# Retention heads with Strassen's scheme: another order of DVE's, ACT's and PE's work, and a weight ring whose slots follow one rule

## The chip, the cores and the metric

The kernel runs on one core of a Trainium2 chip. The metric is the device time of one execution in microseconds, the median over several executions. In the profile PE is TensorE (matmuls), DVE is VectorE, ACT is ScalarE, SP is SyncE (which issues the DMAs).

## The reference

One decoder layer in float32 over x of 8 x 100 tokens by 1024, with a context of 722 tokens for each of the 8 batches. Three parts follow one another, each with a residual and a layer norm: retention, cross attention with its own keys and the context's, and a feed-forward of 4096. The change touches retention alone:

```python
q, k = rope(x @ Wq), rope(x @ Wk)            # 8 heads of 128
v, g = x @ Wv, x @ Wg                        # 8 heads of 256
scores = einsum('bihd,bjhd->bhij', q * scale, k) * D    # D: causal decay of the head
o = einsum('bhij,bjhd->bihd', scores, v)
o = o * rsqrt(mean(o * o) + EPS) * g_norm_weight        # over a head's 256
o = o * (g * sigmoid(g))
x = layernorm(x + o.reshape(B, T, 2048) @ Wo)
```

## The kernel before, in words

Everything is held with its features in the partitions and the 800 tokens side by side. Each float32 operand is split into a high part, rounded by ACT, and a low part, value minus high part, made by DVE. A product is then three matmuls for each 128 x 128 piece of weights: high by high, high by low, low by high.

`phase_retention` works through eight heads. Head 0 (`first_head`) and head 7 (`last_head`) multiply by plain units: 1024 x 128 weights by all 800 tokens, 48 matmuls, in two column parts of 512 and 288. Heads 1 to 6 (`head(i)`) take the weights of q and k, of v, and of g as three blocks (j = 0, 1, 2) of 1024 x 256, and multiply each by Strassen's scheme with seven products (`product(i, j, p)`, p = 0 to 6) over quarters of 512 x 128 weights and 400 tokens, 12 matmuls each. To this belong:

- **Sides.** Four of the seven moving operands are sums of quarters of x. They are made once, in the first head and at the start of head 1: `side_sum(n)` on DVE (L1207), `side_hi(n)` on ACT (L917), `side_lo(n)` on DVE (L1212). Product 1 uses side 2, product 2 side 1, product 3 side 3 and product 5 side 4. Side 4 lies where the upper right quarter of x was (`operand(0, 1)`), so that quarter is restored for head 7, by loading it again (tile QKR), a copy on ACT (L1077) and a low part on DVE (L1449).
- **Weights.** `mix` (DVE, L1165) makes the four weight sums of a block. `entry_hi` (ACT, L878) and `entry_lo` (DVE, L1133) split one quarter of weights into a slot of a ring of four, which is the same memory as the two plain slots WH and WL. An entry is numbered e: 25 to a head, of which 7 for q and k, 7 for v, 4 of the output weights, 7 for g. Its copy waits until PE is done with the entry that had the slot before. From entry 139 (the first output weights of head 6) on, the slots are shifted by two, and entries 139 and 140 wait for entries 137 and 138.
- **Combinations.** PE adds some products up in PSUM; `keep` (ACT, L897), `first_quarter` (ACT, L910) and `combine` (DVE, L1191) make the four quarters of the result: u2, u3, c22, c21, c12, in this order. Their semaphore is `outs`. Product 3 waits for u2, product 5 for u3, product 6 for c22.
- **The head's output.** `weigh_rows` lies between matmuls of block 2. ACT squares and scales the rows (`token_squares` L957, `scaled_rows` L969), PE turns them back (`turn_back`, L1595), DVE multiplies by norm and gate (`gated_output`, L1320), ACT and DVE split (L951, L1310). All of this belongs to head i - 1 and runs at the start of head i. `project_output` (PE, L1519 to L1521) multiplies by the output weights, eight tiles n, through two pairs of PSUM banks; from n = 2 on it waits until DVE's `add_output` (L1260) has added tile n - 2 to the residual R.
- **Rotations** of q and k: `rotate_cos` (L1233), `rotate_sin` (L1238), `rotate_sum` (L1246), between the products of block 1.

Each engine executes its own list in the order in which it is written; nothing is reordered. The order of `head` in `vector` is therefore what decides which of DVE's results comes first: for i > 1 it reads c12 of the head before, low parts 3 and 4, mix 3, u2, low part 5, mixes 0 and 1 of block 1, low part 6, gated output, u3, c22. Before that, at the end of head i - 1, stand low parts 0, 1 and 2.

In the last head PE first waits for c12 of head 6 (`outs`), then runs the first unit (L1723 to L1725) into banks 0 and 1, for each column part first the four pieces of x's lower half and then the four of the restored upper half. On DVE the restored low part (L1449) stands ahead of c12.

Of the kernel before, what the change touches and what calls it, by code (L numbers as in the profile page):

```python
# [682 lines left out]
def phase_retention(c, nc, sem, before, norm):  # L683


    with ExitStack() as ctx:
# [59 lines left out]
        JUMP = PER * (STRASSEN - 1) + OUTPUT_ENTRY  # L746
# [3 lines left out]
        def slot(e):  # L750
            return (e + (2 if e >= JUMP else 0)) % RING

        def slot_users(e):

            return e - 2 if JUMP <= e < JUMP + 2 else e - 4

# [106 lines left out]
        def scalar(act):  # L863
            def plain_hi(u):
                split_hi(c, act, u)

            def entry_hi(e, source, pair, sums):

                before_it = slot_users(e)
                if before_it < 0:  # L870
                    act.wait_ge(c.unit_done, 5 if e < 2 else 6)
                else:
                    act.wait_ge(f_done, F_DONE + before_it + 1)
# [39 lines left out]
            def side_hi(n):  # L913
                act.wait_ge(t_sum, T_SUM + n)
                if n == 3:
                    act.wait_ge(c.unit_done, 6)
# [59 lines left out]
            def first_head():  # L976
# [5 lines left out]
                for t in range(2):  # L982
                    plain_hi(U_RET + WV + t + 2)
# [10 lines left out]
                token_squares(0, 1)  # L994
                act.wait_ge(c.unit_done, 6)
# [18 lines left out]
            def head(i):  # L1014
# [5 lines left out]
                if i == 1:  # L1020
                    side_hi(4)
                    side_hi(3)
# [6 lines left out]
                output_hi(i - 1)  # L1029
                product_hi(i, 1, 0)  # L1030
                first_quarter(i, 0)
                product_hi(i, 1, 1)
# [35 lines left out]
                root(i)  # L1068
                scaled_rows(i)
# [3 lines left out]
            def last_head():  # L1073
                i, u = END, U_END_HEAD
                act.wait_ge(x_back, X_BACK + 16)
                act.wait_ge(f_done, F_DONE + LAST_ENTRY)
                act.activation(operand(0, 1)[0], F1, ACT.Copy).then_inc(t_hi, 1)  # L1077
# [42 lines left out]
        def vector(dve):  # L1120
# [4 lines left out]
            def plain_lo(u):  # L1125
                split_lo(c, dve, u)

# [39 lines left out]
            def combine(i, j, which):  # L1167
# [10 lines left out]
                if which == "u2":  # L1178
                    dve.wait_ge(kept, KEPT + m + 1)
                    if j == 0:  # L1180
                        dve.wait_ge(t_lo, T_LO + 4)
# [27 lines left out]
            def side_lo(n):  # L1209
                dve.wait_ge(t_hi, T_HI + {1: 1, 2: 2, 4: 3, 3: 4}[n])  # L1210
# [114 lines left out]
            def first_head():  # L1325
# [4 lines left out]
                for t in range(2):  # L1330
                    plain_lo(U_RET + WV + t + 2)
# [10 lines left out]
                product_lo(1, 0, 1)  # L1342
                side_lo(2)
                side_sum(4)
                side_sum(3)
# [3 lines left out]
            def head(i):  # L1349
                if i > 1:  # L1350
                    combine(i - 1, 2, "c12")
                    product_lo(i, 0, 3)
                    product_lo(i, 0, 4)
                    mix(i, 0, 3)
                    combine(i, 0, "u2")
                    product_lo(i, 0, 5)
                    mix(i, 1, 0)
                    mix(i, 1, 1)
                    product_lo(i, 0, 6)
                    gated_output(i - 1)  # L1360
                else:
                    product_lo(i, 0, 4)
                    mix(i, 0, 3)
                    side_lo(4)
                    side_lo(3)
                    combine(i, 0, "u2")
                    gated_output(i - 1)
                    product_lo(i, 0, 5)
                    mix(i, 1, 0)
                    mix(i, 1, 1)  # L1370
                    product_lo(i, 0, 6)
                combine(i, 0, "u3")
                combine(i, 0, "c22")
# [12 lines left out]
                mix(i, 1, 3)  # L1386
                rotate_sin(i, 0, 0)
                combine(i, 1, "u2")
# [54 lines left out]
                if i < STRASSEN:  # L1443
                    product_lo(i + 1, 0, 2)

            def last_head():
                i, u = END, U_END_HEAD
                dve.wait_ge(t_hi, T_HI + 5)
                dve.tensor_tensor(operand(0, 1)[1], F1, operand(0, 1)[0].bitcast(F32),  # L1449
                                  ALU.subtract).then_inc(t_lo, 1)  # L1450
                combine(STRASSEN, 2, "c12")
# [60 lines left out]
        def tensor(pe):  # L1512
# [109 lines left out]
            def product(i, j, p):  # L1622
# [23 lines left out]
                if m == 0 and p in (1, 2, 3, 5):  # L1646
                    pe.wait_ge(t_lo, T_LO + {1: 2, 2: 2, 5: 3, 3: 4}[p])
# [24 lines left out]
            def first_head():  # L1672
# [16 lines left out]
                weights(u + WG)  # L1689
                unit_matmuls(c, pe, 0, 6, XH, XL)  # L1690
                weights(u + WG + 1)
                pe.wait_ge(s_masked, 1)
                unit_matmuls(c, pe, 1, 0, XH, XL,
                             lambda h, k: weigh_rows(0, k) if h == 0 else None)

            def head(i):
                for p in range(PRODUCTS):
                    product(i, 0, p)
                    if p == 2:
# [1736 lines left out]
```

## Time and profile before

| | |
|---|---|
| runs | 2728.45, 2728.88, 2729.19 us; median 2728.88 |
| profiled execution | 2728.11 us; its span from first to last instruction 2726.3 us |
| mean granted clock of TensorE | 0.995 of full speed |
| busy DVE, ACT | 62%, 43% of the span |
| retention | from about 550 us to 1152 us of the span |

The rows further down come from several views. The page gives the busy time of each engine. The table of waits says which engine waited for whose result, with the sum, the count and the longest. The view by stretch gives busy time with the number of instructions, the granted clock, and what the DMAs moved. A timeline lists an engine's instructions in the order of time: start, duration, engine, line, operation, output <- inputs, shapes, count; in square brackets the time for which the engine idled just before it, and whom it then waited for.

### The profile page before, as it was taken

What the parts mean: (1) busy time and instruction counts of PE and PEld (TensorE: products, weight loads), DVE (VectorE), ACT (ScalarE), POOL (GpSimd) and SP (SyncE); (2) the same over time, 40 slices, a digit from 0 to 9 for tenths busy, and PEclk for the clock granted to TensorE, in tenths of its full rate; (3) what the DMA queues carried; (4) which work ended last, traced back from release to release, by engine and by line L of the source; (5) the groups of instructions that cost most, each with busy time, mean ns of one, the idle gap of its engine ahead of it and who ended that gap; (6) DMA issues with size and microseconds to landing.
All of it is one profiled execution on the core that took longest, in us unless ns stands there. A gap on an engine that the chain in (4) does not pass through costs nothing. (4 is left out here: it accounts for less than half of the span.)

```text
span 2726.3 us, 39732 instructions
## 1 busy us (share of the span) xinstructions
PE 2666.2 (98%) x15130; PEld 2480.9 (91%) x15130; DVE 1701.0 (62%) x2369; ACT 1162.8 (43%) x2036; POOL 0.9 (0%) x9
## 2 busy tenths in 40 slices
PE   8999999999999998999999999999999999999997
PEld 7888888988999998998889999989999998999997
DVE  4333333368777776558778888845983673773767
ACT  4344444444444443335456666632541341431432
POOL 0000000000000000000000000000000000000000
PEclk9999999999999999999999999999999999999999
DMA  5433333421111111206125555522121121121222
GB/s 209 131 131 131 131 131 131 172 74 56 55 63 63 63 47 59 78 31 143 62 96 167 170 168 168 156 60 99 62 78 62 62 78 62 62 78 49 76 89 100
DMA packets 117224, 265.98 MB, mean 98 GB/s; under 512 B 19822, under 2 KB 86254, under 8 KB 102894
## 3 DMA queue, kind: packets, MB, share of 16 engines
q1 hardware_dynamic: 117102, 264.31, 30.3%
q8 instruction: 82, 1.34, 0.2%
q14 instruction: 40, 0.33, 0.0%
HBM read 206.63 MB, written 57.66 MB: 97 GB/s over the span
## 5 line engine op out<-in xcount | busy, mean ns | idle before, releaser
L129 PE MATMUL PS<-XH,WH 128*128 128x512 f32 (+1 forms) x624 | 215.4, 345 | 0.5 <-DVE t_ROOM L2960 0.4
L131 PE MATMUL PS<-XH,WL 128*128 128x512 f32 (+1 forms) x624 | 215.4, 345 | 0.0
L2816 ACT ACTIVATE WH<-RAW 128x512 fp32r<-128x512 f32 x180 | 113.3, 631 | 222.1 <-PE PS L2692 119.8
L444 PE MATMUL PS<-CH,KWH 128*128 128x338 f32 (+1 forms) x512 | 167.8, 328 | 12.4 <-DVE CL L420 12.4
L3049 DVE TENSOR_TENSOR WL<-RAW,WH 128x512 fp32r<-128x512 f32 x196 | 134.8, 688 | 58.5 <-ACT WH L2816 55.2
L130 PE MATMUL PS<-XL,WH 128*128 128x512 f32 (+1 forms) x496 | 170.1, 343 | 0.0
L445 PE MATMUL PS<-CL,KWH 128*128 128x338 f32 (+1 forms) x512 | 167.6, 327 | 0.0
L446 PE MATMUL PS<-CH,KWL 128*128 128x338 f32 (+1 forms) x512 | 167.5, 327 | 0.0
L2690 PE MATMUL PS<-XL,WH 128*128 128x400 f32 x480 | 166.0, 346 | 0.0
L2688 PE MATMUL PS<-XH,WH 128*128 128x400 f32 x480 | 164.8, 343 | 0.8 <-issue 0.6
L2692 PE MATMUL PS<-XH,WL 128*128 128x400 f32 x480 | 165.1, 344 | 0.0
L2418 DVE TENSOR_TENSOR XL<-PS,XH 128x400 fp32r<-128x400 f32 (+2 forms) x224 | 122.6, 571 | 58.2 <-ACT XH L2357 53.9
L89 ACT ACTIVATE WH<-RAW 128x1024 fp32r<-128x1024 f32 x57 | 60.4, 1061 | 230.9 <-PE PS L131 178.1
L368 DVE TENSOR_TENSOR VS<-PS,VS 128x512 fp32r<-128x512 f32 (+1 forms) x48 | 33.1, 689 | 191.0 <-ACT VS L282 191.0
L470 PE MATMUL PS<-VWH,CL 128*128 128x512 f32 (+1 forms) x384 | 150.0, 391 | 0.0
L469 PE MATMUL PS<-VWH,CH 128*128 128x512 f32 (+1 forms) x384 | 150.0, 391 | 0.0
L471 PE MATMUL PS<-VWL,CH 128*128 128x512 f32 (+1 forms) x384 | 149.6, 390 | 0.0
L2357 ACT ACTIVATE XH<-PS 128x400 fp32r<-128x400 f32 (+2 forms) x224 | 106.2, 506 | 99.2 <-PE PS L2268 97.4
L95 DVE TENSOR_TENSOR WL<-RAW,WH 128x1024 fp32r<-128x1024 f32 x58 | 70.9, 1224 | 121.7 <-ACT WH L89 117.3
L878 ACT ACTIVATE WH<-RAW 128x512 fp32r<-128x512 f32 x132 | 81.7, 633 | 126.1 <-PE PS L1662 69.7
L2725 PE MATMUL PS<-t_ROOM,WL 128*128 128x512 f32 (+1 forms) x384 | 132.5, 345 | 0.0
L2401 DVE TENSOR_REDUCE a_LOW<-PS 100x1 f32<-100x824 f32 x128 | 129.8, 1014 | 4.2 <-PE PS L2257 1.6
(404 smaller groups left out, 7610.8 us busy)
## 6 DMA issues: line engine op xcount, KB each, us to landing
RAW<-weights_dram SPq DMA_DIRECT2D x111, 1024.0 KB, 4.9
values_scratch<-VS SPq DMA_DIRECT2D x40, 512.0 KB, 7.2
a_KHL<-keys_scratch SPq DMA_DIRECT2D x32, 411.0 KB, 5.0
keys_scratch<-KS SPq DMA_DIRECT2D x16, 768.0 KB, 6.2
R<-context_dram SPq DMA_DIRECT2D x8, 1352.0 KB, 6.8
keys_scratch<-KS SPq DMA_DIRECT2D x16, 676.0 KB, 5.5
R<-context_dram SPq DMA_DIRECT2D x7, 1536.0 KB, 6.9
XH<-values_scratch SPq DMA_DIRECT2D x16, 640.0 KB
```

The source lines that it names most:

```text
L129: pe.matmul(out, wh, xh[:, k, cols], start=(k == 0), stop=False)
L130: pe.matmul(out, wh, xl[:, k, cols], start=False, stop=False)
L131: mm = pe.matmul(out, wl, xh[:, k, cols], start=False, stop=(k == KT - 1))
L444: pe.matmul(out, wh, CH[e][:, k, 0:w], start=(k == 0), stop=False)
L445: pe.matmul(out, wh, CL[e][:, k, 0:w], start=False, stop=False)
L446: mm = pe.matmul(out, wl, CH[e][:, k, 0:w], start=False, stop=(k == KT - 1))
L469: pe.matmul(out, ch, vwh[:, k, :], start=(k == 0), stop=False)
L470: pe.matmul(out, cl, vwh[:, k, :], start=False, stop=False)
L471: mm = pe.matmul(out, ch, vwl[:, k, :], start=False, stop=(k == KT - 1))
L2688: pe.matmul(out, wh, high[:, k, :], start=(OPENS[p] and k == 0), stop=False, skip_group_check=True)
L2690: pe.matmul(out, wh, low[:, k, :], start=False, stop=False, skip_group_check=True)
L2692: mm = pe.matmul(out, wl, high[:, k, :], start=False, stop=(k == QUAD - 1), skip_group_check=True)
```

## The change

- **First head.** ACT and DVE split the two gate units in the other order, unit 1 into slot 0 first, unit 0 into slot 1 second. PE multiplies by unit 0 from slot 1 first and waits for both. Side 3's sum comes ahead of side 2's low part, its copy ahead of the second gate's activation, its low part still in the first head.
- **Ring.** Slots are (e + 2) mod 4 for all entries, and each entry waits for the one four before it.
- **Head 1.** u2 is DVE's first operation. Side 4's low part is the only one left. Then low part 5, u3, c22, the gated output, mixes 0 and 1 of block 1, low part 6. PE turns head 0's output back after product 3, no longer after product 2. ACT copies that output later.
- **Heads 2 to 6.** c12 of the head before comes ahead of low part 2. The gated output follows u2, and then come low part 5, u3, c22, the mixes, low part 6. In block 1 u2 comes ahead of the first half of `rotate_sin`.
- **Last head.** ACT copies the restored quarter between the root and the scaling of head 6's rows. DVE makes c12 ahead of the restored low part. PE runs the unit's four pieces that need nothing restored first, right columns (bank 1) and then left ones (bank 0), waits for c12 only ahead of the left ones, and then the four restored pieces in the same order.

Context is shortened here.

```diff
@@ -743,16 +743,11 @@
         LAST_ENTRY = PER * STRASSEN - 1
-        JUMP = PER * (STRASSEN - 1) + OUTPUT_ENTRY
         ring = [x[:].rearrange("p u (s w) -> p (u s) w", s=2) for x in (c.WH, c.WL)]
...
         def slot(e):
-            return (e + (2 if e >= JUMP else 0)) % RING
-
-        def slot_users(e):
-
-            return e - 2 if JUMP <= e < JUMP + 2 else e - 4
+            return (e + 2) % RING
 
@@ -864,13 +859,19 @@
 
+            def first_gate_hi(t):
+
+                u = U_RET + WG + t
+                act.wait_ge(c.raw[(u // 2) % 2], raw_count(u // 2))
+                act.wait_ge(c.unit_done, WG - t)
+                act.activation(c.WH[:, 1 - t, :], raw_unit(c, u), ACT.Copy).then_inc(c.w_hi, 1)
+
             def entry_hi(e, source, pair, sums):
 
-                before_it = slot_users(e)
-                if before_it < 0:
+                if e < RING:
                     act.wait_ge(c.unit_done, 5 if e < 2 else 6)
                 else:
-                    act.wait_ge(f_done, F_DONE + before_it + 1)
+                    act.wait_ge(f_done, F_DONE + e - RING + 1)
                 if sums is not None:
@@ -912,7 +913,7 @@
                 act.wait_ge(t_sum, T_SUM + n)
-                if n == 3:
+                if n == 4:
                     act.wait_ge(c.unit_done, 6)
@@ -980,7 +981,7 @@
                 for t in range(2):
-                    plain_hi(U_RET + WV + t + 2)
+                    first_gate_hi(1 - t)
                     act.activation(halves(VT[:, t, :]), row800(c, 4 + 2 * t),
@@ -992,6 +993,7 @@
                 token_squares(0, 1)
+                side_hi(3)
                 act.wait_ge(c.unit_done, 6)
@@ -1019,16 +1021,18 @@
                     side_hi(4)
-                    side_hi(3)
                 else:
...
                 product_hi(i, 0, 6)
-                output_hi(i - 1)
+                if i > 1:
+                    output_hi(i - 1)
                 product_hi(i, 1, 0)
                 first_quarter(i, 0)
+                if i == 1:
+                    output_hi(i - 1)
                 product_hi(i, 1, 1)
@@ -1066,15 +1070,16 @@
                 root(i)
+                if i == STRASSEN:
+                    act.wait_ge(x_back, X_BACK + 16)
+                    act.wait_ge(f_done, F_DONE + LAST_ENTRY)
+                    act.activation(operand(0, 1)[0], F1, ACT.Copy).then_inc(t_hi, 1)
                 scaled_rows(i)
...
                 i, u = END, U_END_HEAD
-                act.wait_ge(x_back, X_BACK + 16)
-                act.wait_ge(f_done, F_DONE + LAST_ENTRY)
-                act.activation(operand(0, 1)[0], F1, ACT.Copy).then_inc(t_hi, 1)
                 plain_hi(u + 1)
@@ -1125,6 +1130,11 @@
 
+            def first_gate_lo(t):
+                dve.wait_ge(c.w_hi, U_RET + WG + 2 - t)
+                dve.tensor_tensor(c.WL[:, 1 - t, :], raw_unit(c, U_RET + WG + t),
+                                  c.WH[:, 1 - t, :].bitcast(F32), ALU.subtract).then_inc(c.w_lo, 1)
+
             def entry_lo(e, source):
@@ -1178,7 +1188,7 @@
                     if j == 0:
-                        dve.wait_ge(t_lo, T_LO + 4)
+                        dve.wait_ge(t_lo, T_LO + 3)
                     if j == 1:
@@ -1207,7 +1217,7 @@
             def side_lo(n):
-                dve.wait_ge(t_hi, T_HI + {1: 1, 2: 2, 4: 3, 3: 4}[n])
+                dve.wait_ge(t_hi, T_HI + n)
                 high, low = side(n)
@@ -1328,7 +1338,7 @@
                 for t in range(2):
-                    plain_lo(U_RET + WV + t + 2)
+                    first_gate_lo(1 - t)
                 mask_scores(0)
@@ -1340,37 +1350,37 @@
                 product_lo(1, 0, 1)
+                side_sum(3)
                 side_lo(2)
                 side_sum(4)
-                side_sum(3)
+                side_lo(3)
                 product_lo(1, 0, 2)
...
                     combine(i - 1, 2, "c12")
+                    product_lo(i, 0, 2)
                     product_lo(i, 0, 3)
...
                     combine(i, 0, "u2")
+                    gated_output(i - 1)
                     product_lo(i, 0, 5)
-                    mix(i, 1, 0)
-                    mix(i, 1, 1)
-                    product_lo(i, 0, 6)
-                    gated_output(i - 1)
+                    combine(i, 0, "u3")
+                    combine(i, 0, "c22")
                 else:
+                    combine(i, 0, "u2")
                     product_lo(i, 0, 4)
...
                     side_lo(4)
-                    side_lo(3)
-                    combine(i, 0, "u2")
+                    product_lo(i, 0, 5)
+                    combine(i, 0, "u3")
+                    combine(i, 0, "c22")
                     gated_output(i - 1)
-                    product_lo(i, 0, 5)
-                    mix(i, 1, 0)
-                    mix(i, 1, 1)
-                    product_lo(i, 0, 6)
-                combine(i, 0, "u3")
-                combine(i, 0, "c22")
+                mix(i, 1, 0)
+                mix(i, 1, 1)
+                product_lo(i, 0, 6)
                 product_lo(i, 1, 0)
@@ -1384,8 +1394,8 @@
                 mix(i, 1, 3)
+                combine(i, 1, "u2")
                 rotate_sin(i, 0, 0)
-                combine(i, 1, "u2")
                 product_lo(i, 1, 5)
@@ -1440,15 +1450,13 @@
                 combine(i, 2, "c21")
-                if i < STRASSEN:
-                    product_lo(i + 1, 0, 2)
 
...
                 i, u = END, U_END_HEAD
+                combine(STRASSEN, 2, "c12")
                 dve.wait_ge(t_hi, T_HI + 5)
...
                                   ALU.subtract).then_inc(t_lo, 1)
-                combine(STRASSEN, 2, "c12")
                 plain_lo(u + 1)
@@ -1644,7 +1652,7 @@
                 if m == 0 and p in (1, 2, 3, 5):
-                    pe.wait_ge(t_lo, T_LO + {1: 2, 2: 2, 5: 3, 3: 4}[p])
+                    pe.wait_ge(t_lo, T_LO + {1: 2, 2: 2, 3: 3, 5: 4}[p])
                 if e == LAST_ENTRY:
@@ -1686,17 +1694,16 @@
                 turn(0)
-                weights(u + WG)
-                unit_matmuls(c, pe, 0, 6, XH, XL)
                 weights(u + WG + 1)
+                unit_matmuls(c, pe, 1, 6, XH, XL)
                 pe.wait_ge(s_masked, 1)
-                unit_matmuls(c, pe, 1, 0, XH, XL,
+                unit_matmuls(c, pe, 0, 0, XH, XL,
                              lambda h, k: weigh_rows(0, k) if h == 0 else None)
...
                     product(i, 0, p)
-                    if p == 2:
+                    if p == (3 if i == 1 else 2):
                         turn_back(i - 1)
@@ -1711,18 +1718,20 @@
                 weights(u)
-                pe.wait_ge(outs, OUTS + 5 * 3 * STRASSEN)
-                restored = [4, 5, 6, 7, 0, 1, 2, 3]
-                for h in range(2):
-                    cols = slice(*PARTS[h])
-                    out = c.PS[:, h, 0:PARTS[h][1] - PARTS[h][0]]
-                    for n, k in enumerate(restored):
-                        if n == 4:
+                for restored in (False, True):
+                    for h in (1, 0):
+                        if not restored and h == 0:
+                            pe.wait_ge(outs, OUTS + 5 * 3 * STRASSEN)
+                        if restored and h == 1:
                             pe.wait_ge(t_lo, T_LO + 5)
-                        wh, wl = (x[:, u % 2, k * P:(k + 1) * P] for x in (c.WH, c.WL))
-                        pe.matmul(out, wh, XH[:, k, cols], start=(n == 0), stop=False)
-                        pe.matmul(out, wh, XL[:, k, cols], start=False, stop=False)
-                        mm = pe.matmul(out, wl, XH[:, k, cols], start=False, stop=(n == KT - 1))
+                        cols = slice(*PARTS[h])
+                        out = c.PS[:, h, 0:PARTS[h][1] - PARTS[h][0]]
+                        for k in range(0, QUAD) if restored else range(QUAD, KT):
+                            wh, wl = (x[:, u % 2, k * P:(k + 1) * P] for x in (c.WH, c.WL))
+                            pe.matmul(out, wh, XH[:, k, cols], start=(k == QUAD), stop=False)
+                            pe.matmul(out, wh, XL[:, k, cols], start=False, stop=False)
+                            mm = pe.matmul(out, wl, XH[:, k, cols], start=False,
+                                           stop=(k == QUAD - 1))
                 mm.then_inc(c.unit_done, 1)
```

## Rows read from the trace of the kernel before

**Rows 1.** The page: busy time, share of the span and instructions of each engine.
```profile
PE 2666.2 (98%) x15130; PEld 2480.9 (91%) x15130; DVE 1701.0 (62%) x2369; ACT 1162.8 (43%) x2036; POOL 0.9 (0%) x9
```
**Rows 2.** PE's waits, whole span: for whom, us in total, times, longest.
```profile
PE PS L1658 <- DVE QKR L1191: 6.9, 6, 4.7
PE PS L1723 <- DVE G L1191: 5.0, 1, 5.0
PE PS L1519 <- DVE R L1260: 3.3, 1, 3.3
...
PE PS L1658 <- DVE W L1191: 2.3, 5, 0.5
PE PS L1859 <- DVE h_SQL L2025: 2.3, 1, 2.3
...
PE PS L1658 <- DVE G L1191: 1.3, 5, 0.3
```
**Rows 3.** Busy time by stretch: length, PE, PEld, DVE, ACT, POOL, clock, DMA share, GB/s.
```profile
620.00:622.00 2.00, 0.00 (x0) 0.00 (x0) 2.00 (x2) 1.27 (x3) 0.00 (x0) 0.51 0.00 0
...
627.13:649.09 21.96, 21.96 (x121) 21.82 (x121) 19.96 (x29) 8.48 (x14) 0.00 (x0) 1.00 0.29 97
...
1022.00:1024.00 2.00, 0.00 (x0) 0.00 (x0) 1.97 (x4) 0.34 (x1) 0.00 (x0) 1.00 0.00 0
...
1077.69:1103.91 26.22, 26.22 (x148) 23.15 (x146) 16.06 (x16) 6.36 (x8) 0.00 (x0) 1.00 0.12 41
...
1412.00:1414.00 2.00, 2.00 (x8) 1.66 (x7) 1.66 (x3) 1.97 (x3) 0.00 (x0) 0.50 0.75 285
```
**Rows 4.** Timeline of DVE, head 1.
```profile
618.84 1.82 DVE L1212 TENSOR_TENSOR XL<-T,XH 128x1600 fp32r<-128x1600 f32 x1
...
622.53 0.57 DVE L1191 TENSOR_TENSOR QKR<-U,PS 128x400 f32<-128x400 f32 x1
623.02 2.00 DVE L1320 SCALAR_TENSOR_TENSOR G<-PS,GNW,G 128x800 f32<-128x800 f32 x2
...
628.64 0.68 DVE L1133 TENSOR_TENSOR WL<-RAW,WH 128x512 fp32r<-128x512 f32 x1
...
637.14 0.69 DVE L1133 TENSOR_TENSOR WL<-RAW,WH 128x512 fp32r<-128x512 f32 x1 [0.77 <-ACT WH L878]
```
**Rows 5.** Timeline of DVE, head 2.
```profile
697.02 0.69 DVE L1133 TENSOR_TENSOR WL<-RAW,WH 128x512 fp32r<-128x512 f32 x1 [2.72 <-ACT WH L878]
...
703.03 0.69 DVE L1133 TENSOR_TENSOR WL<-RAW,WH 128x512 fp32r<-128x512 f32 x1 [0.31 <-ACT WH L878]
...
725.88 0.98 DVE L1260 TENSOR_TENSOR R<-R,PS 128x800 f32<-128x800 f32 x1
```
**Rows 6.** Timeline of PE: turn backs, third projection tile of head 2.
```profile
616.91 1.59 PE L1595 MATMUL PS<-ID,W 100*128 100x100 f32 x16 [0.59 <-ACT W L969]
...
695.72 1.54 PE L1595 MATMUL PS<-ID,W 100*128 100x100 f32 x16
...
727.01 0.47 PE L1519 MATMUL PS<-VHL,WH 128*128 128x512 f32 x1
...
1076.38 0.85 PE L1595 MATMUL PS<-ID,W 100*128 100x100 f32 x8
```
**Rows 7.** Timeline of DVE, output weights of head 6.
```profile
1015.52 0.69 DVE L1133 TENSOR_TENSOR WL<-RAW,WH 128x512 fp32r<-128x512 f32 x1 [3.19 <-ACT WH L878]
```
**Rows 8.** Timelines of DVE and ACT, start of the last head.
```profile
1062.55 1.83 DVE L1449 TENSOR_TENSOR XL<-QKR,XH 128x1600 fp32r<-128x1600 f32 x1 [3.20 <-ACT XH L1077]
1064.29 0.56 DVE L1191 TENSOR_TENSOR G<-G,PS 128x400 f32<-128x400 f32 x1
...
1058.07 3.02 ACT L969 ACTIVATE W<-PS,RSS 100x256 f32<-100x256 f32 x8
1060.93 1.58 ACT L1077 ACTIVATE XH<-QKR 128x1600 fp32r<-128x1600 f32 x1
```

## The prediction

> **What bounds the kernel now.** I read the page first, then the table of PE's waits, then the busy time by stretch, and last the timelines of single engines around each wait. The page [rows 1] says that PE is busy 98% of the span, so only its idle time, or time at a lower clock, can be won: the change removes no matmul. The table of waits [rows 2] puts 18.8 us of that idle time in retention, in five rows: 6.9 us at L1658 for QKR (six waits, the longest 4.7), 5.0 once at L1723 (the last head), 3.3 once at L1519 (the output projection), 2.3 in five small waits for W and 1.3 in five for G. Clock: in the stretches [rows 3] the granted clock is 0.51 (its 1.2 GHz level) right after the long wait of head 1 and 1.00 (2.4 GHz) in the middle of the 3.3 us wait. So the 4.7 and 5.0 us waits also cost time at half clock.
>
> The second thing to see is in the DVE timeline: between a head's turned-back output and its first row sums (L1260) DVE works nearly without a gap. In head 2 the first such sum ends at 725.88 + 0.98 = 726.86 [rows 5] and the third projection matmul group starts at 727.01 [rows 6], 0.15 later, which is the latency of a semaphore. So **once per head DVE's queue, not PE, sets the time**. Small PE waits removed before that point come back there, unless DVE also gets there earlier. I assume that head 1 and heads 3 to 6 are alike; the code of that stretch is the same.
>
> **Head 1.** The third product ends at 616.91 - 0.59 = 616.32 [rows 6]. PE then turns head 0's output back (1.59 us) and waits 4.7 us, up to 623.2, since product 3 needs u2, which DVE makes at 622.53 behind the low parts of side 4 (618.84) and side 3 [rows 4]. The new order makes side 3's sum, high and low part inside the first head, ahead of the low part of entry 2, which there waits for ACT's second gate; I price that at nothing, and at one low part (1.82 us) if this cover were gone. u2 comes first in the head. Product 3 then starts at 616.3 at once and the turn back follows it. The stretch from product 4's start at 627.13 holds ten products in 21.96 us [rows 3], 2.2 each (product 3, at half clock, took 627.13 - 623.2 = 3.9 or 4.0: 1.8 more). Now PE ends product 3 at 618.5, the turn back at 620.0, product 4 at 622.2 and product 5 at 624.4. DVE: side 4's low part starts at 618.84 as before. Side 3's is gone from there (622.53 - 618.84 - 1.82 = 1.87 us), and so is u2 (623.02 - 622.53 = 0.49). The operations up to the next block's first low part are otherwise the same ones in another order, so that one starts at 628.64 - 2.36 = 626.3. The low part of product 6 stands right before it, behind the gated output and two mixes, and PE has wanted it since 624.4: **a new wait of 1.9 us**. Later the 0.77 us that DVE idled for ACT at 637.14 [rows 4] goes too, because ACT's copy there follows PE's product, which now ends some 5 us earlier. DVE reaches the first row sum 2.36 + 0.77 = 3.1 us earlier, and PE, which has more in hand than that, waits there. Term: **3.1 us**, out of the 0.6 + 4.7 + 1.8 = 7.1 that the waits and the clock cost; PE keeps 7.1 - 1.9 - 3.1 = 2.1 us in hand at the row sum.
>
> **Heads 2 to 6.** The third quarter of the block before (c12) is put ahead of a low part, which removes PE's 0.26 us wait for G (1.3 in five) [rows 2]. The turn back of head 2 ends at 695.72 + 1.54 = 697.26 [rows 6], so now at 697.0. The gated output now starts there instead of the low part of product 5, which waited for ACT until 697.02 [rows 5]. Up to the low part at 703.03 the operations are the same ones, without the 0.31 us idle before it, as the gated output is finished sooner and ACT's copies of it with it. DVE gains 0.31 + 0.04 = 0.35 us per head, 5 x 0.35 = **1.75 us**. That u3 no longer stands behind the gated output (6.9 - 4.7 = 2.2 in five, 0.44 us of PE's wait per head, in the QKR row) and u2 no longer behind a rotation (0.46, the W row) I price at nothing: this time comes back at the row sum, which covers it. Were that cover gone, it would be 0.44 + 0.46 per head, 4.5 in five.
>
> **Ring without a skip.** Slots are now (entry + 2) mod 4 throughout. Before, entries 14 and 15 of head 6 had to wait for the product two entries back. DVE idled 3.19 us for that at 1015.52 [rows 7] and PE waited 3.3 us at L1519 [rows 2]. Both go: **3.3 us**. To match, the first head's two gate units change slots, with copies and low parts at the same places behind the same waits, but PE now wants both before the first. No row shows that wait. Its bounds are 0 and one low part, which is at most the 1.82 us of the longer one at 618.84 [rows 4]; I take 0, as the scores and transposes lie between the second low part and the gates on PE.
>
> **Last head.** PE ends the Strassen products at about 1060.0: c12 ends at 1064.29 + 0.56 = 1064.85 [rows 8], 0.15 of latency, less the 5.0 us wait. Its restored unit then runs to 1076.38 [rows 6], 16.4 us in all, where three units of this shape take 26.22 us [rows 3], 8.74 each. After the change nothing holds PE: the halves over the unrestored rows stand first, the first of them in a bank that nobody still reads, so it starts at 1060.0. The second needs c12, which DVE now makes as soon as the last product ends (about 1060.7), as it no longer queues behind L1449. The restored part needs L1449's result. ACT's copy for it now stands ahead of the scaling (1058.07, 3.02 us), so it is done by 1058.07 + 1.58 = 1059.7, and DVE's by 1060.7 + 1.83 = 1062.5, while PE has half of 8.74 us of work up to 1064.4. The scaling ends by 1062.7, and the turn back wants it at 1068.7. Term: 16.4 - 8.7 = **7.7 us**, 5.0 of them wait and 2.7 clock.
>
> **Other moved steps.** SyncE's load of the output weights waits for the low part of product 6, which in heads 2 to 6 is made some 3 us later, behind the gated output. Seven products (15 us) lie between that and the copies that need it, so I take 0; its bounds are 0 and the 0.77 us for which DVE idled for a copy in rows 4, per head. The load of the next pair and the copies of the gated output move with DVE.
>
> **Sum.** 3.1 + 1.75 + 3.3 + 7.7 = 15.85 us, against the profiled execution's 2728.1 (span 2726.3 and 1.8 around it): 2712.3. The median of the runs is 0.8 higher, so the forecast is **2713.0 us**, -0.6%. About 0.2% (5.5 us) is what a measurement of this kernel can tell from no change.
>
> **Rivals.**
> *The clock falls at the new wait of head 1.* A 2.3 us wait at L1859 [rows 2] was followed by a clock of 0.50 in the stretch from 1412 [rows 3], while the 3.3 us wait of head 6 was not. So 1.9 us can do it. Half clock cost PE 1.8 us in head 1 and 2.7 in the last head, where a full product or unit ran through it; I take up to 3.5 for a drop whose whole length is filled with work. PE has 2.1 us of that in hand before the row sum: 1.4 us, 2714.4. Chance 0.22.
> The Trainium skill's page "TensorE: Matmul & The Clock Gate", Part 1 ("What's actually happening"), says that the monitor behind the clock runs freely and doesn't restart with the kernel. By that a wait near 2 us may or may not lower the clock from run to run; no row here repeats one wait in two executions.
> *All waits go.* DVE keeps up and PE gets back 18.8 us and the clock's 1.8 and 2.7: 23.3 us, 2705.6. Against it speaks the gapless DVE queue up to 726.86. Chance 0.08.
> *The ring gives nothing* because head 6 waits for something else at the same place (the row sums), or the part does not act: 2716.3, and 2720 if c12 also stays late in the last head. Chance 0.09.
> *Slower.* In heads 2 to 6 the low parts of products 5 and 6 now queue behind the gated output, which waits for the turn back and for ACT's gates. Product 6's low part is ready at about 702.7 and PE wants it at 696.8 + 3 x 2.2 = 703.4: 0.7 us in hand. If the gates or the turn back come late, each microsecond past 0.7 is PE's wait in five heads, and the clock may fall as well (1.8 each time, as in head 1). Late by 3 us: 5 x (2.3 + 1.8) = 20.5 us, 2733; slower than before from about 2.2 us on. Against it: ACT finished the copy that the row at 697.02 waited for by then, and the gates stand ahead of that copy on ACT, so they are done some microseconds before 697.0. Chance 0.04.
>
> **How the numbers follow.** The forecast has 0.57. Its own unknowns (0.35 per head by +-0.3, the head 1 term by +-1, latencies) make 2710.5 to 2715.5. The range takes in the clock rival and the missing ring, and half the way to "all waits go": 2708 to 2718. Faster by over 0.2% holds for all cases but the slower one and mishaps in between: 0.93, within 0.2% 0.03, slower 0.04.
>
> **What would show it.** Right: no wait at L1723; no 4.7 us wait, but one of about 2 us at L1658 in head 1 whose releaser is a low part (L1133); new waits at L1519 for R (L1260) of 0.5 to 0.9 us in each of six heads, in place of QKR and W; a granted clock of 1.00 all through the last head's first unit. Wrong: L1519 without waits (then more was won), a wait before product 6 in every head, or waits in the last head's unit.

## The result, and the profile after

The changed kernel takes **2709.01 us** in the median of four runs (2708.18 to 2709.96), the one before 2729.03 (2728.45 to 2729.31): 20.0 us less, ratio 0.9927, 95% interval 0.9910 to 0.9944. The profiled executions stand at 2728.11 and 2709.04, their spans at 2726.3 and 2707.2.

Of after, first the engines in the page, then PE's waits in the whole span (for whom, us in total, times, longest):
```profile
PE 2660.4 (98%) x15130; PEld 2476.9 (91%) x15130; DVE 1700.3 (63%) x2369; ACT 1162.6 (43%) x2036; POOL 0.9 (0%) x9
```
```profile
PE PS L444 <- DVE CL L420: 12.6, 1, 12.6
PE PS L1527 <- DVE R L1270: 2.5, 5, 0.5
...
PE PS L1666 <- DVE WL L1143: 2.1, 1, 2.1
...
PE PS L1666 <- DVE W L1201: 1.0, 5, 0.2
```
The instruction counts are those of [rows 1]; nothing was removed. The first row lies outside retention. Of retention's 18.8 us in [rows 2], 5.6 are left, in the other three rows: the waits for QKR and G are gone, head 6's 3.3 us wait for R has become one of five of 0.5 us, the waits for W are shorter, and a wait for WL is new. DVE releases all of them. Lines have moved: L1133 is L1143 now, L1191 L1201, L1260 L1270, L1519 L1527, L1658 L1666, L1723 L1731.

The time is best followed from one first row sum to the next, since that operation occurs once per head. DVE's timeline after:
```profile
614.14 0.57 DVE L1201 TENSOR_TENSOR QKR<-U,PS 128x400 f32<-128x400 f32 x1
...
618.78 1.83 DVE L1222 TENSOR_TENSOR XL<-T,XH 128x1600 fp32r<-128x1600 f32 x1
622.28 2.00 DVE L1330 SCALAR_TENSOR_TENSOR G<-PS,GNW,G 128x800 f32<-128x800 f32 x2
...
625.53 1.29 DVE L1143 TENSOR_TENSOR WL<-RAW,WH 128x512 fp32r<-128x512 f32 x2
...
648.98 0.98 DVE L1270 TENSOR_TENSOR R<-R,PS 128x800 f32<-128x800 f32 x1
...
693.49 2.01 DVE L1330 SCALAR_TENSOR_TENSOR G<-PS,GNW,G 128x800 f32<-128x800 f32 x2 [2.84 <-PE PS L1603]
...
698.50 1.29 DVE L1143 TENSOR_TENSOR WL<-RAW,WH 128x512 fp32r<-128x512 f32 x2
...
721.95 0.98 DVE L1270 TENSOR_TENSOR R<-R,PS 128x800 f32<-128x800 f32 x1
...
1013.68 0.98 DVE L1270 TENSOR_TENSOR R<-R,PS 128x800 f32<-128x800 f32 x1
...
1050.19 0.57 DVE L1201 TENSOR_TENSOR G<-G,PS 128x400 f32<-128x400 f32 x1 [0.70 <-PE PS L1670]
1050.68 1.82 DVE L1458 TENSOR_TENSOR XL<-QKR,XH 128x1600 fp32r<-128x1600 f32 x1
```
and PE's:
```profile
626.36 0.52 PE L1666 MATMUL PS<-XH,WH 128*128 128x400 f32 x1 [2.14 <-DVE WL L1143]
...
691.85 1.54 PE L1603 MATMUL PS<-ID,W 100*128 100x100 f32 x16
...
1049.99 0.29 PE L1731 MATMUL PS<-XH,WH 128*128 128x288 f32 x1
...
1058.71 0.34 PE L1603 MATMUL PS<-ID,W 100*128 100x100 f32 x2
```
For before, beside [rows 5, 6]:
```profile
652.35 0.98 DVE L1260 TENSOR_TENSOR R<-R,PS 128x800 f32<-128x800 f32 x1
```
The first row sums of heads 1 to 6 stood at 652.35, 725.88, 799.40, 872.97, 946.54 and 1023.55 before, and stand at 648.98, 721.95, 794.88, 867.82, 940.75 and 1013.68 after. From these and the first turn back of the last head (1076.38 before, 1058.71 after):

| stretch | before | after | gain | forecast |
|---|---|---|---|---|
| to row sum of head 1 | 652.35 | 648.98 | 3.37 | 3.1 |
| row sums 1 to 2, 2 to 3, 3 to 4, 4 to 5 | 73.53, 73.52, 73.57, 73.57 | 72.97, 72.93, 72.94, 72.93 | 0.56 to 0.64 | 0.35 each |
| row sums 5 to 6 | 77.01 | 72.93 | 4.08 | 0.35 + 3.3 |
| row sum 6 to last turn back | 52.83 | 45.03 | 7.80 | 7.7 |

These are 17.67 us. The other 1.4 of the span's 19.1 lie behind retention, where the change has no part, and they are luck: before, the granted clock fell once more near 1774; after, it did not. The changed kernel was profiled a second time ("The changed kernel once more", below), and there it did. Before, after, and the same place in that second execution (length, PE, PEld, DVE, ACT, POOL, clock, DMA share, GB/s):
```profile
1774.00:1776.00 2.00, 2.00 (x9) 1.78 (x9) 1.03 (x2) 0.80 (x2) 0.00 (x0) 0.50 0.91 46
```
```profile
1774.00:1776.00 2.00, 2.00 (x10) 1.66 (x9) 2.00 (x3) 0.00 (x0) 0.00 (x0) 1.00 0.00 0
```
```profile
1758.00:1760.00 2.00, 2.00 (x10) 1.86 (x9) 1.09 (x2) 0.72 (x2) 0.00 (x0) 0.50 0.91 70
```

### The profile page after: what moved, and what is told of

Same layout as the page of the kernel before. It is cut to its first block and busy times, and to the rows that moved or that the text cites. A ratio compares the mean times of both kernels' runs of the same rounds, so it can differ in the third digit from the quotient of the medians.

```text
span 2707.2 us, 39730 instructions
## 1 busy us (share of the span) xinstructions
PE 2660.4 (98%) x15130; PEld 2476.9 (91%) x15130; DVE 1700.3 (63%) x2369; ACT 1162.6 (43%) x2036; POOL 0.9 (0%) x9
```

## The experiments

### Four parts, one at a time, on the kernel before

**The last head alone**: c12 ahead of L1449's low part, ACT's copy ahead of the scaling, unrestored rows first. Of the edit only DVE's part is shown.
```diff
+                combine(STRASSEN, 2, "c12")
                 dve.wait_ge(t_hi, T_HI + 5)
                 dve.tensor_tensor(operand(0, 1)[1], F1, operand(0, 1)[0].bitcast(F32),
                                   ALU.subtract).then_inc(t_lo, 1)
-                combine(STRASSEN, 2, "c12")
```


> The kernel before with the last head's part alone: PE runs the unrestored pieces first, DVE makes c12 ahead of the restored low part, ACT copies the restored quarter ahead of the scaling. Theory (the last head's stall is local, all of it goes): -7.8 us against before, 2721.2, of which 5.0 is the wait at L1723 and the rest the clock; no clock of 0.5 around 1064. Rival (part of it comes back in the unit behind, for instance as a wait for the rotations or the turn back): -5 us or less, 2724. The stretches at half clock further down (at 1412 and 1774 in before) may come or go and are worth up to 1.7 us each.


Measured: 2723.77 us against 2729.07, ratio 0.9977 (0.9967 to 0.9986). The unit itself shrank to 8.72 us as forecast (1064.61 to 1073.33). But the profiled execution lost time elsewhere. Its busy time by stretch at head 6's 3.3 us wait for the row sums (columns as in [rows 3]):
```profile
1026.00:1028.00 2.00, 1.22 (x3) 1.05 (x4) 2.00 (x3) 1.16 (x2) 0.00 (x0) 0.50 0.00 0
1028.00:1030.00 2.00, 2.00 (x7) 1.61 (x7) 1.04 (x2) 0.00 (x0) 0.00 (x0) 0.50 0.88 225
```
The clock fell at a wait that had left it at 1.00 in the profiled execution of before [rows 3], and the way from that row sum to the unit's start took 38.96 us instead of 36.29 (before without its 5.0 us wait), 2.7 more. The ten runs form two groups, four at 2720.5 to 2721.4 and six at 2723.7 to 2724.8, some 3 us apart. That the upper group is the one whose clock falls there fits, but only one of the ten, of the upper group, has a trace.

**The ring alone**: slots (e + 2) mod 4, with the first head's gate units exchanged.
```diff
         def slot(e):
-            return (e + (2 if e >= JUMP else 0)) % RING
...
+            return (e + 2) % RING
```


> The kernel before with the ring without a skip and the swapped gate units alone. Theory (head 6 then behaves like heads 2 to 5): the 3.3 us wait at L1519 goes, head 6 takes 73.6 us from row sum to row sum in place of 77.0: -3.4 us, 2725.6. Rival (the row sums hold PE at the same place anyway, or the gate units cost a wait in the first head): 0 to -1 us.


Measured: 2724.80, ratio 0.9984 (0.9975 to 0.9994). The step to head 6's row sum is 73.54 instead of 77.01, **3.5 us** less, L1519's wait is gone, and the others stand as in [rows 2], these two among them:
```profile
PE PS L1664 <- DVE QKR L1197: 6.9, 6, 4.7
PE PS L1728 <- DVE G L1197: 5.0, 1, 5.0
```
The exchanged gate units show no wait. The median moved by 4.3, 0.8 more than this stretch. In the profiled execution the last head's unit and its half clock took 10.20 us from start to turn back (1063.33 to 1073.53) where before took 11.38 (1065.00 to 1076.38), with the same 5.0 us wait ahead: the length of a drop varies too.

**The first head alone**: side 3 made ahead, u2 first, PE's product 3 ahead of the turn back.
```diff
                 token_squares(0, 1)
+                side_hi(3)
...
                     side_hi(4)
-                    side_hi(3)
```


> The kernel before with head 1's part alone: sides in the order 1, 2, 3, 4 with side 3 in the first head, u2 first, turn back behind product 3, gated output behind c22. Theory (DVE's queue sets the time): the first row sum of head 1 comes 3.3 us earlier (649.0 in place of 652.35), with a wait of 2.1 us before product 6; -3.3 us, 2725.7. Rival (PE sets the time): the 4.7 and 0.6 us waits and the 1.8 us of half clock go, 2.1 come back: -5.0 us, 2724.


Measured: 2725.34, ratio 0.9987 (0.9978 to 0.9997). PE's first turn back and DVE's row sum:
```profile
618.73 0.25 PE L1601 MATMUL PS<-ID,W 100*128 100x100 f32 x1
...
649.42 0.98 DVE L1263 TENSOR_TENSOR R<-R,PS 128x800 f32<-128x800 f32 x1
```
They are 30.69 us apart, as after the whole change (618.29 to 648.98), with the same 2.1 us wait for WL.

**The order of heads 2 to 6 alone.**
```diff
                     combine(i - 1, 2, "c12")
+                    product_lo(i, 0, 2)
...
                     combine(i, 0, "u2")
+                    gated_output(i - 1)
                     product_lo(i, 0, 5)
+                    combine(i, 0, "u3")
+                    combine(i, 0, "c22")
                     mix(i, 1, 0)
                     mix(i, 1, 1)
                     product_lo(i, 0, 6)
-                    gated_output(i - 1)
...
```


> The kernel before with the order of heads 2 to 6 alone (and u2 ahead of the first rotation half in block 1 of every head). Theory (DVE's queue sets the time; the turn back comes 0.5 us earlier and DVE's 0.31 us idle time goes): heads 2 to 5 take 72.95 us each in place of 73.5, row sums wait 0.5 us at L1519; head 6 keeps its ring wait; -3.0 to -3.8 us, 2725.6. Rival (as forecast, 0.35 per head): -1.75 us. Rival (PE sets the time): 1.2 per head, -6 us.


Measured: 2726.23, ratio 0.9990 (0.9981 to 1.0000). Row sums are 72.94, 72.92, 72.94 and 72.93 apart, so this part alone gives the 0.6 us per head; head 6, still with its ring wait, takes 75.70 (77.01 before: 1.3 less). The 2.2 of QKR and 1.3 of G are gone, and 5.4 - 3.3 = 2.1 stand at the row sums:
```profile
PE PS L1520 <- DVE R L1260: 5.4, 5, 3.3
```
In this execution too the clock fell at head 6's 3.3 us wait:
```profile
1022.00:1024.00 2.00, 2.00 (x6) 1.52 (x6) 1.49 (x2) 0.00 (x0) 0.00 (x0) 0.50 0.69 131
```
The way from that row sum to the unit's start, without the 5.0 us wait ahead of it, took 38.97 us, 2.7 more than before, as with the last head alone. In the profiled execution of the first head alone, the fastest of its ten, the same wait left the clock at 1.00.

The four medians add to 5.3 + 4.3 + 3.7 + 2.8 = 16.1 us of the 20.0. By the stretch that each part changes, the traces add to 7.8 (last head) + 3.5 (ring) + 3.3 (head 1, turn back and row sum counted from the first turn back of the kernel) + 3.8 (heads 2 to 6: 2.5 up to head 5, 1.3 in head 6) = 18.4, against 17.7 for all together. The 0.7 between these is head 6, where the order alone gives 1.3 and the ring alone 3.5, but both together 4.1. So in the traces the parts add up where they act, and what the medians lack lies elsewhere. The drop at head 6's wait is 2.7 us of it in two of the four traces; in how many of the runs without a trace it came is not shown.

### The new wait of the first head

**Product 6's low part ahead of the gated output.**
```diff
                     combine(i, 0, "c22")
+                    product_lo(i, 0, 6)
                     gated_output(i - 1)
...
```


> The changed kernel with the low part of product 6 of head 1 put ahead of the gated output. Theory (DVE's queue sets head 1's time, PE has time in hand): the 2.1 us wait before product 6 goes and with it the stretch at half clock around 627, a wait of about 0.6 us appears before the next block's first product, and the first row sum stays where it is, 30.7 us after the turn back's start: 0 us. Rival (the wait and the clock are on the path): -2 to -3.8 us.


Measured: 2709.37 (2707.75 and 2710.99), ratio 0.9925 (0.9897 to 0.9954). PE's waits in retention, and both marks:
```profile
PE PS L1529 <- DVE R L1270: 3.0, 6, 0.5
PE PS L1668 <- DVE W L1201: 2.6, 7, 1.3
PE PS L1668 <- DVE WL L1143: 0.9, 2, 0.5
```
```profile
618.15 0.25 PE L1605 MATMUL PS<-ID,W 100*128 100x100 f32 x1
...
648.84 0.98 DVE L1270 TENSOR_TENSOR R<-R,PS 128x800 f32<-128x800 f32 x1
```
Again 30.69 us. The wait did not go; it split up. PE now waits 0.55 us ahead of product 6, and later 0.37, 1.33 (for u2 of block 1) and 0.21: 2.5 us in all before the row sum, where the next execution has 2.7 at the same full clock (2.14 + 0.39 + 0.21). So this run shows that the place of the wait is worth 0.00; it does not show what the wait's length is worth. The clock stayed at 1.00.

**The changed kernel once more**, for the clock at that wait.


> The changed kernel once more, beside the next one and timed more often: 2709, -20 us against before. Theory (the clock falls or doesn't at the same wait from run to run): its runs spread over some 2 us; rows: row sum to row sum 72.93.


Measured: 2710.80 (five runs, 2709.48 to 2712.99) against 2728.87, ratio 0.9930 (0.9917 to 0.9944). In its profiled execution the same wait left the clock alone. By stretch, first the changed kernel's first profiled execution, then this one:
```profile
626.00:628.00 2.00, 1.64 (x5) 1.65 (x6) 1.51 (x3) 0.36 (x1) 0.00 (x0) 0.63 0.50 66
628.00:630.00 2.00, 2.00 (x8) 1.99 (x8) 1.70 (x3) 0.79 (x2) 0.00 (x0) 0.51 0.92 385
```
```profile
627.00:629.00 2.00, 1.20 (x7) 1.23 (x8) 1.95 (x4) 0.00 (x0) 0.00 (x0) 1.00 0.31 45
629.00:631.00 2.00, 2.00 (x13) 2.00 (x12) 1.26 (x2) 1.79 (x3) 0.00 (x0) 1.00 0.84 328
```
The timelines of PE and DVE in this execution:
```profile
619.73 0.25 PE L1603 MATMUL PS<-ID,W 100*128 100x100 f32 x1
...
627.80 0.42 PE L1666 MATMUL PS<-XH,WH 128*128 128x400 f32 x1 [2.14 <-DVE WL L1143]
...
650.42 0.98 DVE L1270 TENSOR_TENSOR R<-R,PS 128x800 f32<-128x800 f32 x1
```
2.14 us both times, half clock once, and 619.73 to 650.42 is 30.69 in spite of it. What the lower clock took from PE shows in the waits behind it. At full clock PE waits three more times in head 1, up to and including the row sum: 0.39 and 0.21 us for W and 0.51 for R. At half clock it doesn't. So the drop took at least these 1.1 listed us from PE, and the row sum did not move: PE had them in hand. Four more traces have the same wait, the drop and 30.66 to 30.70 us: the first head alone, the extra operation behind, c12 put back and the mixes ahead, all in this document.

### Is it DVE's queue?

One more DVE operation of 0.98 us, whose result nothing uses, was put once per head ahead of the row sums, and in another kernel behind them.
```diff
+            def extra(i):
+                dve.tensor_reduce(GAP[:, 8 * i:8 * i + 8], cos, AX.X, ALU.max)
...
                 product_lo(i, 1, 4)
+                extra(i)
```
(the second kernel has `extra(i)` behind `product_lo(i, 2, 6)` instead.)


> The changed kernel with one more DVE operation per head, a maximum over 128x800 values into an unused tile (about 1 us), in block 1 behind low part 4, between the turn back and the first row sum. Theory (DVE's queue sets the time there): each of heads 1 to 6 takes as much longer as the operation lasts, about 1.0 us: row sum to row sum 73.9 in place of 72.93, +6 us in all, and the wait at the projection grows from 0.5 to about 1.4. Rival (PE sets it): 0 to +0.3 per head.

> The changed kernel with the same extra operation per head, but in block 2 behind low part 6, where DVE idles 2.3 us for PE. Theory: hidden, row sum to row sum 72.93 as before, 0 us. Rival (DVE's total work sets the time): +1.0 per head, +6 us.


Ahead: 2714.89, ratio 0.9947 (0.9924 to 0.9969), row sums 73.68 to 73.72 apart, **0.75 us per head more**. Behind: 2709.78, ratio 0.9931 (0.9908 to 0.9954), row sums 72.91 to 72.95 apart, **0**. DVE of the first, then of the second:
```profile
708.21 0.98 DVE L1152 TENSOR_REDUCE GAP<-COS 128x8 f32<-128x800 f32 x1
...
723.56 0.98 DVE L1274 TENSOR_TENSOR R<-R,PS 128x800 f32<-128x800 f32 x1
```
```profile
675.37 0.98 DVE L1152 TENSOR_REDUCE GAP<-COS 128x8 f32<-128x800 f32 x1
677.73 1.25 DVE L1205 TENSOR_TENSOR G<-G,PS 128x400 f32<-128x400 f32 x2 [1.37 <-PE PS L1675]
```
DVE still idles 1.37 us behind the operation in the back; in the front it has little to spare. The engine is 63% busy in both. The expected 0.98 was too much: the next operation starts 0.89 after this one (708.21 to 709.10), and the 0.14 between 0.89 and 0.75 would be slack that the queue still had; where it lay is not shown. The time also did not show where it was expected: the wait for R stayed at 0.5, and the waits for W ahead of it grew from 1.0 (5) to 4.7 (10).

**c12 put back behind a low part**, the rest as changed.
```diff
-                    combine(i - 1, 2, "c12")
                     product_lo(i, 0, 2)
+                    combine(i - 1, 2, "c12")
```


> The changed kernel with c12 of the head before put back behind low part 2 in heads 2 to 6. Theory (PE's wait for c12, told as 0.26 us, costs 0.5 with the slower start of the matmuls behind it; the turn back comes that much later and DVE's queue starts with it): row sum to row sum 73.4 in place of 72.93, +2.4 us in all. Rival (the cost is the listed wait): 73.2, +1.3 us. Rival (the start of the gated output doesn't depend on it): 72.93, 0 us.


Measured: 2712.43, ratio 0.9942 (0.9919 to 0.9964), row sums 73.44 to 73.48 apart, 0.52 per head more, for a wait that is listed as 0.26:
```profile
PE PS L1666 <- DVE G L1201: 1.3, 5, 0.3
```
What such a wait costs is seen in PE's timeline of before, ahead of product 1 of head 2:
```profile
690.64 0.35 PE L1662 MATMUL PS<-XH,WL 128*128 128x400 f32 x1
691.24 0.45 PE L1658 MATMUL PS<-SIDE,WH 128*128 128x400 f32 x1 [0.26 <-DVE G L1191]
691.53 0.35 PE L1660 MATMUL PS<-SIDE,WH 128*128 128x400 f32 x1
```
Matmuls of this shape start every 0.18 us when nothing holds them (21.96 us for 120 of them [rows 3]). Here the next starts 0.60 behind the last (0.42 lost), the one after 0.29 behind that (0.11 more): 0.53. The list counts only from the last matmul's modelled end, 0.35 after its start. The fifteen small waits of heads 2 to 6 of before all look like this: 0.53 lost for 0.26 listed, and 0.71 to 0.75 for 0.44 to 0.47, so 1.99 us per head for 1.16 listed.

### A better order

**Mixes 0 and 1 ahead of the gated output** in heads 2 to 6, to shorten what stands between the turn back and the row sums. DVE makes them while it idles for the turn back.
```diff
                     combine(i, 0, "u2")
+                    mix(i, 1, 0)
+                    mix(i, 1, 1)
                     gated_output(i - 1)
```


> The changed kernel with mixes 0 and 1 of block 1 (1.33 us of DVE) moved in heads 2 to 6 from behind c22 to behind u2, where DVE idles 2.8 us for the turn back. Theory (DVE's queue from the turn back to the first row sum sets the head's time): the row sum comes 1.3 us earlier as far as PE can follow, so the 0.5 us wait at the projection and the 0.2 us waits for W go; a head takes about 72.0 us from row sum to row sum in place of 72.93, -4.5 us in all. Rival (DVE's queue doesn't matter any more, the waits left are latencies): 72.9, no change.


Measured: 2703.08 (2702.51 and 2703.64), ratio 0.9902 (0.9874 to 0.9931); row sums 71.63 or 71.64 apart, **1.3 us per head less** than the changed kernel, where 0.9 was expected. All that is left of PE's waits in retention:
```profile
PE PS L1668 <- DVE WL L1143: 2.1, 1, 2.1
```
**The first head too**: ACT's copies of entry 4 and of side 4 ahead of the scaling, both mixes ahead of side 4's low part.
```diff
                 keep(1, 0)
+                product_hi(1, 0, 4)
+                side_hi(4)
                 scaled_rows(0)
...
                     mix(i, 0, 3)
+                    mix(i, 1, 0)
+                    mix(i, 1, 1)
                     side_lo(4)
```


> The changed kernel with e5's edit, and in head 1 two more: ACT copies entry 4 and side 4 ahead of head 0's scaling, and DVE makes the two mixes of block 1 before side 4's low part, in the 2.7 us for which it idled for ACT. Theory (DVE's queue sets the time up to the first row sum): in head 1 DVE's low part of block 1's product 0 starts 2.3 us earlier (at about 623.8 in place of 626.1), the wait of 2.1 us before product 6 goes, the turn back starts 0.6 us later; the row sum comes 2.3 us earlier than in e5. With e5's 6.5 us: -8.8 us against the changed kernel, 2700.3. Rival (PE has no more in hand in head 1, or the later turn back holds DVE): as e5, 2703.


Measured: **2702.16** (2701.31 to 2702.73) against 2728.87, ratio 0.9900 (0.9885 to 0.9915); the changed kernel took 2710.80 against the same runs of before. The first row sum stands at 647.62, and the kernel's first turn back came 1.19 us later than in the changed kernel's profile (588.70 and 587.51), so 2.5 us are won there, and the waits in retention shrink to 0.9 us:
```profile
PE PS L1529 <- DVE R L1270: 0.5, 1, 0.5
PE PS L1605 <- ACT W L970: 0.4, 1, 0.4
```

## Why the prediction was right, and where it was not

The result lies within the range, 4.0 us below the forecast. It is also 1.5 us below the 2710.5 to 2715.5 that the forecast's own unknowns should have covered; it is in the range because that was drawn wider towards a rival. Of the 4.0 us, 1.8 are terms of the sum, 1.4 the clock near 1774 and 0.8 the difference between profiled executions and medians. The last two are chance: in its second set of runs the changed kernel stood at 2710.80, 18.1 us under before.

- **What bounds the kernel** was right, with a limit. An operation of 0.98 us costs 0.75 per head in front of the row sums and nothing behind them; moving PE's 2.1 us wait there gives 0.00, and a clock drop that took at least 1.1 us from PE costs 0.00. What the prediction did not say is where the stretch begins: at the turn back, which starts the gated output. Ahead of it PE sets the time, so PE's waits there count in full (with c12 late the turn back came 0.51 us later after the row sum before it, and the next row sum 0.52). One reading was off: the stretch 620 to 622 [rows 3] lies inside the long wait of head 1 (PE busy 0.00), not right after it; the clock stayed at 0.50 up to 626, so what was read from it holds.
- **Head 1**: 3.4 for 3.1, right in its steps too, but for what PE kept in hand: at full clock it waits a listed 1.1 us up to the row sum, not 2.1 (about 1.9 with 0.26 more for each of three waits). The wait before product 6 came at 626.36 for 626.3, with 2.14 us for 1.9 and the low part as its releaser; u2 was ready at 614.14 + 0.57, ahead of product 3, and side 4's low part started at 618.78 for 618.84.
- **Heads 2 to 6: the failed step.** "DVE gains 0.31 + 0.04 = 0.35 us per head" was 0.61 in the mean ((0.56 + 0.59 + 0.63 + 0.64 + 0.64) / 5, with head 6 taken as head 5), 3.06 for 1.75 in all. The wait for G was taken at its listed 0.26; its removal is worth 0.50 to 0.53. The 0.04 does not follow from the rows either: a turn back that ends at 697.00 is 0.02 ahead of 697.02. Counted back from the row sum before, the turn back of head 2 came 43.37 us later before (695.72 - 652.35) and 42.87 after (691.85 - 648.98), DVE's queue behind the turn back (before the low part of product 5, now the gated output) started 44.67 and 44.51 later (0.16 won, 0.04 forecast), and the next block's first low part 50.68 and 50.12 (0.56 won): 0.16, the 0.31 of idle time, and about 0.1 of a denser queue. The other terms priced at nothing, u3 and u2, did come back at the row sum, as the 0.5 us waits for R, five in this execution (head 1's is missing) and six in the second; the 0.2 us waits for W in five heads were not forecast.
- **Ring**: 4.08 - 0.64 = 3.4 for 3.3 (3.5 alone). **Last head**: 16.54 us from the last product to the turn back became 8.72, 7.8 for 7.7; no wait at L1731, and the clock at 1.00:
```profile
1050.00:1052.00 2.00, 2.00 (x15) 1.95 (x14) 1.81 (x2) 2.00 (x6) 0.00 (x0) 1.00 0.00 0
```
- **Sum**: 17.7 in retention for 15.85; 1.3 of that gap is heads 2 to 6, 0.5 the three other terms. The remaining 1.4 of the span is the clock near 1774, which no term held. The medians differ by 0.9 more than the spans (20.0 and 19.1), since before's profiled execution was 0.9 below its median of all four runs.
- **Rivals.** The clock did fall at head 1's new wait in the profiled execution, but its price of 1.4 us was wrong: PE had enough in hand for it, and the row sum came at the same 30.69 us with it and without. The Trainium skill's page "TensorE: Matmul & The Clock Gate", Part 1, says that the monitor behind the clock runs freely. The two executions with one 2.14 us wait and two clocks fit that; they do not show it. "All waits go" was not this change, but the experiments reached it in heads 2 to 6: 71.64 us per head, 1.9 below before. There the three kinds of wait of before (0.26, 0.44 and 0.46 per head, 1.16 listed) are worth 73.54 - 71.64 = 1.90, close to the 1.99 that the starts of the matmuls show. The slower case did not come: no wait before product 6 outside head 1.

## What to carry to other kernels

The share of busy time doesn't tell whether an engine's in-order queue sets the time: find the point where its last operation and the next one of the busiest engine touch, then ask what starts that stretch. Here PE's waits counted in full ahead of the start, and not at all inside the stretch while PE had time in hand. The way on was to move DVE's work out of the stretch (two mixes moved: 2703.1 for the changed kernel's 2709.0), not to remove more waits. An operation without use, put once on either side of the point, tests this for the price of a run.

## What the runs showed of the hardware that was not expected

- A short wait costs PE about 0.27 us more than the list of waits shows: 0.26 listed, 0.50 to 0.52 measured when it was removed and put back, 0.53 by the starts of the matmuls. Of that, 0.16 lies in how the list counts (from a modelled end), and 0.11 is the matmul after the one that waited, which starts 0.29 behind it and not 0.18.
- The same wait does not always lower the clock. The 2.14 us wait of head 1 stands in seven of the traces; in six the 1.2 GHz level followed, in one (the changed kernel's second profiled execution) the clock stayed at 2.4 GHz, and one of the six is the same kernel's first execution. Head 6's 3.3 us wait stands in four: the clock fell in two (the last head alone, the order alone; 2.7 us lost each) and stayed in two (before, the first head alone). A 2.3 us wait behind retention (L1859 in before) stands in all thirteen: the clock fell in nine. The executions were not all on one chip, and the runs give no cause, so which of the two comes stays open. A wait that costs only its length in one trace may cost more in the next run.
